# Last FFN of a cross-attention block: half of the output product ahead, scores from unscaled rows, ranks read from PSUM, the landing awaited in the second block

## The chip, the cores and the metric

The kernel runs on one core of one Trainium2 chip. The metric is the device time in microseconds, the median of three runs. All times below are of one launch on one core.

## The reference

The reference is one transformer layer on 8 batches of 512 rows of 256 numbers, float32, in two parts.

```python
x = x + xattn(layernorm(x), ctx, ctx, mask)      # 16 heads of 16, 1024 keys, softmax, then @ w_o.T
x = x + ffn(layernorm(x))

# ffn(y), for each batch:
scores = y @ w_router                 # one number per row
_, idx = top_k(scores, 128)           # the 128 best rows of the batch
x_sel = y[idx]
h = rmsnorm(x_sel, g1); qkv = h @ W_qkv.T        # 16 heads, causal attention over the 128 rows
x_attn = softmax(q k.T / 4 + causal) v @ W_out.T
h2 = rmsnorm(x_sel + x_attn, g2)
x_ff = (silu(h2 @ W1.T) * (h2 @ W2.T)) @ W3.T    # 682 wide
out = y with rows idx set to x_sel + x_attn + x_ff
```

So a batch goes through attention, an output product with w_o, a residual sum (x1), a layer norm of x1 (y), a score and a rank for each row, a gather of 128 rows, a small attention and a gated product, and an add of the 128 new rows onto their places in the output.

## The kernel before

Batches are pipelined by hand. The attention of batch b runs in 32 steps; each step has a score product on TensorE (L439), two exponentials on ScalarE (L469) and a value product (L458). Between the steps stand, by tables that name a step for each piece (`PE_SLOT`, `ACT_SLOT`, `DVE_ORDER`), the projections of batch b+1 and the pieces of the FFN of batch b-1. There the FFN has one PSUM bank for itself, bank 7, called `MISC`.

After the attention of the last batch nothing is left to hide its FFN behind. It runs as a chain of pieces, in the order of `PE_FFN`, `ACT_FFN`, `DVE_FFN` and `POOL_FFN`, with banks from `BANK_LAST`. The pieces, each named by a string, are:

- `wo0`, `wo1`: the output product. Each waits for both halves of `o_t` (the transposed attention output, two halves of 128 channels, L551), makes two of the four row tiles, and VectorE adds them to x1 (L615), takes statistics (L619) and aggregates them (L623).
- GpSimd `var`: two small instructions (L763, L765) that make the reciprocal standard deviation `rstd2`.
- `y`: VectorE subtracts the mean and multiplies by `rstd2` (L629), then multiplies by the router's weights with a running sum (L633), which gives `score`.
- `spread`: TensorE transposes the scores so that every partition holds all 512 (L247); ScalarE copies them to `all_scores` in SBUF (L496).
- `rank0` to `rank3`: VectorE counts for each row the rows ahead of it (L643, L646) and makes the selection (L605). Ahead of them stand three instructions that check denominators (L974 to L979).
- `gather`, `hidT`, `kq`, `v`, `fs`, `pv`, `wout`, `hid2T`, `u0`, `w0`, `u1`, `w1`, `down`: gather of 128 rows, keys and queries in one bank (L679, L681 read them), values, small attention, and the gated product. `u` goes through tanh on ScalarE (L522) and L716 on VectorE, `w` through L723.
- `add`: GpSimd issues an indirect DMA that adds 128 rows to the output in DRAM (L780), and waits for its landing (L782).

`product` (L256) splits a product into four column strips of 32; an fp32 product shows as two instructions for each matmul in the trace. `spare_products` (L266) are products of a constant with itself whose result nobody reads; `SPARE` says how many stand ahead of which piece on TensorE. `take_bank` (L271) waits for a bank.

The program has two blocks. The first, fast one ends with the wait of SyncE for the landing of the last indirect DMA, and all engines meet (L802). In the second each engine loads a flag; if it is set, the whole computation is done again in a general form. Here it isn't set, and the engines branch over the code to the end, where they meet again (L1061).

## Time and profile before

| | |
|---|---|
| median of 3 runs | 920.99 us (918.51, 920.99, 922.82) |
| the profiled execution | 918.08 us |
| its span, first to last instruction | 915.8 us |
| mean granted TensorE clock | 0.995 |
| TensorE busy / VectorE / ScalarE / GpSimd | 95% / 35% / 62% / 10% |
| steps of the last attention end at | 849.45 us |
| last DMA issue on GpSimd | 906.18 to 907.84 us |

About 2.3 us of the profiled execution lie around the span. The shares of busy time are of the whole span; the change touches the last 66 us of it, where TensorE is busy for a good part with spare products. In the page, the digits of TensorE's clock are 9 (0.9 or more of full speed) in all but the last of 40 slices.

### The profile page before, as it was taken

To read this page: it belongs to the slowest core of one execution; us is meant where nothing else is said; L and a number is where in the kernel's file an instruction comes from. 1 tells how busy PE (TensorE), PEld (TensorE's weight loads), DVE (VectorE), ACT (ScalarE), POOL (GpSimd) and SP (SyncE) were. 2 spreads that over 40 slices of the span, in tenths; PEclk is the share of its full clock that TensorE was granted. 3 is DMA by queue.
4 is the path that set the end of the run, shared out by engine and by line. 5 is a ranking of instruction groups with operands and counts; after the bars stand their busy time and mean duration, and the time that the engine had idled before them with its cause. 6 is when DMAs were issued, how large, how long until landed. Compare 5 with 4: busy or idle time off the path is not lost. (4 is left out here: it accounts for less than half of the span.)

```text
span 915.8 us, 28668 instructions
## 1 busy us (share of the span) xinstructions
PE 866.5 (95%) x12040; PEld 305.6 (33%) x12047; DVE 316.4 (35%) x919; ACT 570.8 (62%) x645; POOL 92.7 (10%) x147
## 2 busy tenths in 40 slices
PE   7999999999999999999999999999999999989874
PEld 2322222333333423334323433334323332324443
DVE  2222216331452216331363324532263314421631
ACT  3466777666577666766676666676676667776110
POOL 3100101110000101011101101001011100010011
PEclk9999999999999999999999999999999999999998
DMA  5060201120001200111001200202001100100000
GB/s 179 2 236 1 76 3 25 48 77 8 2 25 48 77 7 25 48 31 48 8 24 48 77 8 2 68 5 78 7 2 47 31 8 1 48 1 5 5 25 9
DMA packets 24955, 33.73 MB, mean 37 GB/s; under 512 B 1231, under 2 KB 22009, under 8 KB 24825
## 3 DMA queue, kind: packets, MB, share of 16 engines
q1 hardware_dynamic: 23672, 30.81, 10.4%
q0 software_dynamic: 1152, 1.05, 1.0%
q8 instruction: 98, 1.61, 0.7%
q14 instruction: 33, 0.26, 0.1%
HBM read 26.61 MB, written 5.24 MB: 35 GB/s over the span
## 5 line engine op out<-in xcount | busy, mean ns | idle before, releaser
L469 ACT ACTIVATE probs<-pair_bank 128x1024 f32<-128x1024 f32 x512 | 496.3, 1021 | 241.2 <-ACTq L468 241.2
L439 PE MATMUL pair_bank<-q_sb,k_sb 32*64 32x512 f32 x4096 | 286.2, 612 | 17.1 <-PEq L436 17.0
L458 PE MATMUL o_bank<-probs,va 128*32 128x512 f32 x2048 | 272.8, 604 | 3.3 <-PEq L455 2.2
L439 PEld LDWEIGHTS pair_bank<-q_sb,k_sb 32*64 32x64 f32 x4096 | 61.3, 129 | 147.2 <-issue 147.1
L458 PEld LDWEIGHTS o_bank<-probs,va 128*32 128x32 f32 x2048 | 41.3, 108 | 207.0 <-issue 122.3
L256 PE MATMUL m_bank<-wv_sb,ctx_in 128*32 128x256 f32 x1024 | 61.3, 379 | 0.4 <-PEq L271 0.4
L256 PE MATMUL m_bank<-ctx_in,wk_sb 128*32 128x512 f32 x480 | 58.1, 592 | 0.0
L542 DVE STREAM_TRANSPOSE o_blk<-o_bank 128x512 f32<-128x512 f32 x32 | 22.9, 717 | 93.8 <-DVEq L541 93.8
L595 DVE TENSOR_SCALAR q_sb<-m_bank,parity 128x512 f32<-128x512 f32 x30 | 21.1, 746 | 81.0 <-DVEq L593 81.0
L256 PEld LDWEIGHTS m_bank<-wv_sb,ctx_in 128*32 128x32 f32 x1024 | 33.9, 110 | 35.8 <-issue 20.4
L583 DVE TENSOR_SCALAR va<-m_bank,valid 128x256 f32<-128x256 f32 x64 | 28.0, 478 | 49.9 <-DVEq L577 49.9
L256 PEld LDWEIGHTS m_bank<-hid_t,w 128*32 128x32 f32 x1392 | 39.3, 110 | 17.3 <-issue 16.6
L256 PE MATMUL m_bank<-hid_t,w 128*32 128x128 f32 x1392 | 43.4, 273 | 0.5 <-PEq L271 0.5
L266 PE MATMUL o_bank<-before 128*128 128x512 bf16 x122 | 29.7, 395 | 3.3 <-POOL before L858 2.7
L615 DVE TENSOR_TENSOR x<-x,m_bank 128x512 f32<-128x512 f32 x14 | 9.6, 688 | 61.2 <-DVEq L614 61.2
L256 PE MATMUL m_bank<-xn_t,wq_sb 128*32 128x512 f32 x240 | 30.7, 592 | 0.0
L477 ACT ACTIVATE k_sb<-m_bank 128x512 f32<-128x512 f32 x30 | 17.9, 597 | 19.4 <-ACTq L476 19.4
L755 POOL TENSOR_TENSOR mask_in<-mask_in,mask_row 128x256 int32<-128x256 int32 x32 | 22.4, 730 | 69.5 <-POOLq L752 69.5
L771 POOL TENSOR_SCALAR_AFFINE_SELECT p_f<-p_f 128x1024 f32<-128x1024 f32 x16 | 17.5, 1091 | 116.4 <-POOLq L769 115.4
L780 POOL DMA_INDIRECT out_dram<-att,row_of x8 | 13.3, 1668 | 150.1 <-POOLq L779 150.1
L256 PEld LDWEIGHTS m_bank<-ctx_in,wk_sb 128*32 128x32 f32 x480 | 15.7, 110 | 35.8 <-issue 35.8
L256 PE MATMUL m_bank<-wo,o_t 128*32 128x256 f32 x448 | 26.7, 379 | 0.0
(164 smaller groups left out, 595.6 us busy)
## 6 DMA issues: line engine op xcount, KB each, us to landing
ctx_in<-in_ctxT SPq DMA_DIRECT2D x8, 1024.0 KB, 5.0
x_in<-in_x SPq DMA_DIRECT2D x8, 512.0 KB, 4.0
x<-in_x SPq DMA_DIRECT2D x8, 512.0 KB, 4.3
mask_in<-in_mask SPq DMA_DIRECT2D x8, 512.0 KB, 3.9
out_dram<-base SPq DMA_DIRECT2D x8, 512.0 KB, 5.2
mask_row<-in_mask SPq DMA_DIRECT2D x8, 128.0 KB, 3.9
wqkv<-in_wqkvT SPq DMA_DIRECT2D x1, 768.0 KB
w<-in_w1T SPq DMA_DIRECT2D x1, 682.0 KB
```

The costliest lines, as they stand in the source:

```text
L256: last = nc.tensor.matmul(dst[j], a[:, j], c, start=(begins and n == 0), stop=(ends and n == len(pairs) - 1))
L266: last = nc.tensor.matmul(dst, before[:, 0, 0:P], before[:, 1], start=True, stop=True)
L439: last = nc.tensor.matmul(pair_bank[pairs[r // 2]][j:j + 64, r % 2], key_tile(b, s, r)[:, j:j + 64], query_tile(b, s, r), start=True, stop ...
L458: last = nc.tensor.matmul(o_bank[32 * r:32 * r + 32], va[b % 2][:, t, HV * h:HV * h + 32], probs[s % 2][:, r], start=(t == 0), stop=(t == ...
L469: nc.scalar.activation(probs[s % 2][:, 2 * e:2 * e + 2, :], pair_bank[p][:], ACT.Exp, scale=HD ** -0.5).then_inc(s_free[p], 1)
L477: nc.scalar.activation(k_sb[b % 2][:, m, half * 512:(half + 1) * 512], bank[i], ACT.Copy).then_inc(bank_free[i], 1)
L542: nc.vector.transpose(o_blk[:], o_bank[:]).then_inc(o_free, 1)
L583: last = nc.vector.tensor_scalar(by_head(va[b % 2][:, t])[:, :, 0:HD], bank[i][:, e * D:(e + 1) * D].rearrange("p (h d) -> p h d", h=H), o ...
L595: last = nc.vector.tensor_scalar(q_sb[b % 2][:, m, par], bank[i], parity[:, par:par + 1], None, ALU.mult)
L755: last = nc.gpsimd.tensor_tensor(mask_words[:, t * WORDS:(t + 1) * WORDS], mask_words[:, t * WORDS:(t + 1) * WORDS], first, ALU.subtract)
L771: last = nc.gpsimd.affine_select(out=half, in_=half, compare_op=ALU.is_ge, fill=0.0, base=0, pattern=[[0, H8], [1, CAP]], channel_multipli ...
L780: nc.gpsimd.indirect_dma_start(out.rearrange("b s d -> (b s) d"), bass.IndirectOffsetOnAxis(row_of[:, 0:1], 0), att[:], None, compute_op=A ...
```

## The change

In the last FFN alone:

- `wo` takes the place of `wo0` and `wo1`. It waits for the first half of `o_t`, multiplies it with all four tiles into four banks, then waits for the second half and completes them. VectorE adds and takes statistics tile by tile.
- `score` takes the place of `y`: the mean is subtracted ahead of the wait for `rstd2`; the score product has `rstd2` as its scalar; then the rows are multiplied by `rstd2`.
- ScalarE's `spread` is gone; the ranks read the bank (bank 4).
- Keys go to one bank and queries to the next, each with a signal of its own (`k,q`); `v` moves to bank 7.
- The gated product goes `u0`, `u1`, `w0`, `w1` rather than `u0`, `w0`, `u1`, `w1`.
- Spare products: ahead of the output product 2 for 12, ahead of `spread` 17 for 24, ahead of `gather` 27 for 36.
- `add` waits for the stored rows first and for the new rows second (this holds for all batches); in the last batch GpSimd no longer waits for the landing, and SyncE waits for it in the second block, between the load of the flag and the branch.

The general form in the second block keeps the old pieces.

```diff
-PE_FFN = ["wo0", "wo1", "spread", "gather", "hidT", "kq", "v", "fs", "pv", "wout", "hid2T", "flag", "u0", "w0", "u1",
+PE_FFN = ["wo", "spread", "gather", "hidT", "k,q", "v", "fs", "pv", "wout", "hid2T", "flag", "u0", "u1", "w0",
-SPARE = {"wo0": 12, "spread": 24, "gather": 36, "hidT": 10, "pv": 14, "wout": 6, "hid2T": 10}
+SPARE = {"wo": 2, "spread": 17, "gather": 27, "hidT": 10, "pv": 14, "wout": 6, "hid2T": 10}
 def pe_ffn(pe, stage, i, part=None):
+    if stage == "wo":
+        pe.wait_ge(o_t_ready, 1)
+        tiles = [take_bank(pe, i + t)[:, 0:D] for t in range(QT)]
+        for t in range(QT):
+            product(tiles[t], [(o_t[:, 0, t * P:(t + 1) * P], wo[:, 0])], ends=False)
+        pe.wait_ge(o_t_ready, 2)
+        pe.sem_inc(o_t_ready, -2)
+        for t in range(QT):
+            product(tiles[t], [(o_t[:, 1, t * P:(t + 1) * P], wo[:, 1])], begins=False).then_inc(done["wo"], 1)
+    elif stage == "k,q":
+        ...
+        for e in range(2):
+            dst = take_bank(pe, i + e)
+            for n in range(2):
+                first = (D if e == 0 else 0) + n * P
+                last = product(dst[:, n * CAP:(n + 1) * CAP],
+                               [(wqkv[:, c, first:first + P], hid_t[:, c]) for c in range(KC)])
+            last.then_inc(done["kq"], 1)
 def dve_ffn(dve, stage, b, i):
+    if stage == "wo":
+        ...
+        for t in range(QT):
+            dve.wait_ge(done["wo"], 1)
+            dve.sem_inc(done["wo"], -1)
+            nc.vector.tensor_tensor(x1[:, t], x1[:, t], bank[i + t][:, 0:D], ALU.add).then_inc(bank_free[i + t], 1)
+            dve.drain()
+            nc.vector.bn_stats(stats2[:, t], x1[:, t])
+        dve.drain()
+        for t in range(QT):
+            nc.vector.bn_aggr(mv2[:, t], stats2[:, t])
+        dve.drain().then_inc(var2_ready, 1)
+    elif stage == "score":
+        for t in range(QT):
+            nc.vector.tensor_scalar(y[:, t], x1[:, t], mv2[:, t, 0:1], None, ALU.subtract)
+        dve.wait_ge(rstd2_ready, 1)
+        dve.sem_inc(rstd2_ready, -1)
+        dve.drain()
+        for t in range(QT):
+            unused = ties[t // 2][:, (t % 2) * D:(t % 2 + 1) * D]
+            nc.vector.scalar_tensor_tensor(out=unused, in0=y[:, t], scalar=rstd2[:, t:t + 1], in1=wr_b[:], op0=ALU.mult,
+                                           op1=ALU.mult, accum_out=score[:, t:t + 1])
+        dve.drain().then_inc(score_ready, 1)
+        for t in range(QT):
+            nc.vector.tensor_scalar(y[:, t], y[:, t], rstd2[:, t:t + 1], None, ALU.mult)
     elif stage in ("rank0", "rank1", "rank2", "rank3"):
+        others = all_scores[:] if i == MISC else bank[i]
+        elif t == 0:
+            dve.wait_ge(done["spread"], 1)
 def pool_ffn(pool, stage, n=None):
     elif stage == "add":
+        pool.wait_ge(base_stored, 16)
+        pool.sem_inc(base_stored, -16)
         pool.wait_ge(delta_ready, 1)
         pool.sem_inc(delta_ready, -1)
-        pool.wait_ge(base_stored, 16)
-        pool.sem_inc(base_stored, -16)
         nc.gpsimd.indirect_dma_start(...).then_inc(added, 16)
-        pool.wait_ge(added, 16 * (n + 1))
-        pool.sem_inc(add_done, 1)
+        if n != B - 1:
+            pool.wait_ge(added, 16 * (n + 1))
+            pool.sem_inc(add_done, 1)
 # SyncE, end of the first block
-                sp.wait_ge(added, 16 * B)
 # SyncE, second block
                 general = sp.value_load(flags_i[0:1, 0:1], min_val=0, max_val=1)
+                sp.wait_ge(added, 16 * B)
                 with sp.If(general == 1):
```

TensorE's order from the end of the last attention (`o_bank<-probs1,va1` is its last value product) to the gather, before. `before` is the constant of the spare products; the number at a row's end counts instructions of one form.

```order
L458 MATMUL o_bank<-probs1,va1 32x512 x4
L266 MATMUL pair_bank0<-before 128x512 x12
L256 MATMUL pair_bank0<-wo,o_t 32x256 x32
L266 MATMUL o_bank<-before 128x512 x24
L247 MATMUL m_bank<-ident,score 128x128 x4
L266 MATMUL o_bank<-before 128x512 x36
L256 MATMUL pair_bank0<-y_tok,sel 32x257 x16
```

And now, on the same engine at the same place:

```order
L478 MATMUL o_bank<-probs1,va1 32x512 x4
L266 MATMUL pair_bank2<-before 128x512 x2
L256 MATMUL pair_bank0<-wo,o_t 32x256 x8
L256 MATMUL pair_bank1<-wo,o_t 32x256 x8
L256 MATMUL pair_bank0<-wo,o_t 32x256 x8
L256 MATMUL pair_bank1<-wo,o_t 32x256 x8
L266 MATMUL o_bank<-before 128x512 x17
L247 MATMUL pair_bank2<-ident,score 128x128 x4
L266 MATMUL o_bank<-before 128x512 x27
L256 MATMUL pair_bank0<-y_tok,sel 32x257 x16
```

The 32 matmuls of the output product are now two passes over four tiles, with the wait for the second half of `o_t` between the passes; 26 spare products of 72 are gone.

VectorE's order from the aggregation of the statistics (L623) to the first rank (L643), before:

```order
L623 BN_AGGR mv2<-stats2 128x2 x4
L629 TENSOR_SCALAR y_tok<-x1,mv2,rstd2 128x256 x4
L633 SCALAR_TENSOR_TENSOR ties0,score<-y_tok,wr_b 128x256 x2
L633 SCALAR_TENSOR_TENSOR ties1,score<-y_tok,wr_b 128x256 x2
L974 TENSOR_SCALAR ties0<-inv_all 128x512
L976 SCALAR_TENSOR_TENSOR ties0,checks<-inv_all,ties0 128x512
L979 TENSOR_REDUCE checks<-differs 128x1
L643 SCALAR_TENSOR_TENSOR ties0,rank<-all_scores,score,before 128x128
```

And now:

```order
L639 BN_AGGR mv2<-stats2 128x2 x4
L644 TENSOR_SCALAR y_tok<-x1,mv2 128x256 x4
L650 SCALAR_TENSOR_TENSOR ties0,score<-y_tok,rstd2,wr_b 128x256 x2
L650 SCALAR_TENSOR_TENSOR ties1,score<-y_tok,rstd2,wr_b 128x256 x2
L654 TENSOR_SCALAR y_tok<-y_tok,rstd2 128x256 x4
L1039 TENSOR_SCALAR ties0<-inv_all 128x512
L1041 SCALAR_TENSOR_TENSOR ties0,checks<-inv_all,ties0 128x512
L1044 TENSOR_REDUCE checks<-differs 128x1
L695 SCALAR_TENSOR_TENSOR ties0,rank<-pair_bank2,score,before 128x128
```

Four instructions that multiply y by `rstd2` have come in between the score and the first rank (L654), and the ranks' input is a bank.

## Rows read from the trace of the kernel before

**Rows 1.** Windows by stage: length, busy time of each engine, granted clock, DMA.

```profile
845.00:916.00 71.00, 49.11 (x628) 26.46 (x634) 26.08 (x82) 8.67 (x14) 7.58 (x10) 0.94 0.06 13
```

**Rows 2.** Timeline, output product: start, length, engine, line, operation; idle time before.

```profile
851.27 0.71 DVE L551 STREAM_TRANSPOSE o_t<-o_nrm 128x512 f32<-128x512 f32 x1
852.28 3.66 PE L256 MATMUL pair_bank<-wo,o_t 128*32 128x256 f32 x64
854.39 0.69 DVE L615 TENSOR_TENSOR x<-x,pair_bank 128x512 f32<-128x512 f32 x1 [2.41 <-DVEq L614]
855.16 0.76 DVE L619 BATCH_NORM_STATS2 stats<-x 128x6 f32<-128x256 f32 x2
...
857.72 0.38 DVE L623 BATCH_NORM_AGGREGATE mv<-stats 128x2 f32<-128x6 f32 x4
```

**Rows 3.** Timeline, normalisation and scores.

```profile
858.80 1.05 POOL L765 TENSOR_TENSOR rstd<-veps,neg_half 128x4 f32<-128x4 f32 x1 [0.24 <-issue]
860.00 1.38 DVE L629 TENSOR_SCALAR y_tok<-x,mv,rstd 128x256 f32<-128x256 f32 x4 [1.90 <-DVEq L627]
861.45 0.43 DVE L633 SCALAR_TENSOR_TENSOR ties<-y_tok,wr_b 128x256 f32<-128x256 f32 x1
...
862.84 0.08 DVE L633 DVE_READ_ACCUMULATOR ties<-y_tok,wr_b 128x1 f32 x1
```

**Rows 4.** Timeline, from the spread scores to the gather.

```profile
863.25 0.62 PE L247 MATMUL m_bank<-ident,score 128*128 128x128 f32 x4 [2.02 <-PEq L271]
...
863.71 7.93 PE L266 MATMUL o_bank<-before 128*128 128x512 bf16 x35
864.00 0.60 ACT L496 ACTIVATE all_scores<-m_bank 128x512 f32<-128x512 f32 x1 [14.63 <-ACTq L495]
...
864.79 0.35 DVE L643 SCALAR_TENSOR_TENSOR ties<-all_scores,score,before 128x128 f32<-128x128 f32 x1 [0.43 <-DVEq L640]
...
869.58 0.77 DVE L605 TENSOR_SCALAR sel<-iota_r,rank 128x128 f32<-128x128 f32 x2
871.57 1.95 PE L256 MATMUL pair_bank<-y_tok,sel 128*32 128x257 f32 x32
```

**Rows 5.** One line's instructions: ns min/median/max, first and last start; forms.

```profile
L580 DVE COPY va<-valid x64: 167/174/706, 23.7 to 668.1; 128x16 f32<-128x16 f32 x64
```

**Rows 6.** Timeline, gathered rows, keys and queries.

```profile
875.88 0.48 DVE L670 SCALAR_TENSOR_TENSOR hid<-x_sel,ms,g_b 128x256 f32<-128x256 f32 x1 [0.55 <-DVEq L669]
...
877.92 1.95 PE L256 MATMUL pair_bank<-hid_t,wqkv 128*32 128x128 f32 x64 [0.84 <-PEq L271]
...
880.04 0.42 DVE L679 COPY k_f<-pair_bank 128x256 f32<-128x256 f32 x1 [2.36 <-DVEq L678]
```

**Rows 7.** Timeline, gated product.

```profile
901.41 3.23 PE L256 MATMUL pair_bank<-w,gate 128*32 128x256 f32 x48
902.03 0.56 DVE L723 SCALAR_TENSOR_TENSOR gate<-pair_bank,silu 128x384 f32<-128x384 f32 x1 [0.30 <-DVEq L722]
```

**Rows 8.** Timeline, the end.

```profile
904.81 0.42 DVE L738 TENSOR_TENSOR att<-att,pair_bank 128x256 f32<-128x256 f32 x1 [2.23 <-DVEq L737]
...
906.18 1.66 POOL L780 DMA_INDIRECT out_dram<-att,row_of  x1 [12.20 <-POOLq L779]
```

**Rows 9.** Single lines of the queues: ns min/median/max, first and last start.

```profile
L783 POOLq EVENT_SEMAPHORE  x8: 17/17/17, 227.9 to 910.1; - x8
...
L1161 POOLq TENSOR_LOAD <-flags_i x1: 504/504/504, 910.5 to 910.5; - x1
...
L1240 PEldq COMPARE_BRANCH  x1: 3927/3927/3927, 911.5 to 911.5; - x1
```

**Rows 10.** Windows of TensorE: length, busy time (instructions), granted clock, DMA.

```profile
904.00:905.00 1.00, 0.64 (x11) 1.00 0.00 0
...
907.00:908.00 1.00, 0.00 (x0) 0.50 0.00 0
```

**Rows 11.** Timeline, the first spare products of the program.

```profile
2.66 3.69 PE L266 MATMUL o_bank<-before 128*128 128x512 bf16 x9 [2.66 <-POOL before L858]
```

More of the change, by code:

```diff
@@ L45 @@
 BANK_FIRST = {"xT0": 0, "xT1": 1, "K00": 2, "Q0": 3, "K01": 4, "valid": MISC}
-BANK_LAST = {"wo0": 0, "wo1": 1, "spread": 7, "gather": 0, "hidT": 7, "kq": 0, "v": 1, "pv": 7, "wout": 0,
+BANK_LAST = {"wo": 0, "spread": 4, "rank0": 4, "rank1": 4, "rank2": 4, "rank3": 4, "gather": 0, "hidT": 7, "k,q": 0, "v": 7, "pv": 7, "wout": 0,
              "hid2T": 1, "flag": 6, "u0": 7, "w0": 0, "u1": 1, "w1": 2, "down": 3}
@@ L78 @@
 POOL_ORDER = [("F", "var"), ("P", "var"), ("F", "rms0"), ("F", "causal"), ("F", "rms1"), ("P", "differ"), ("F", "add")]
-PE_FFN = ["wo0", "wo1", "spread", "gather", "hidT", "kq", "v", "fs", "pv", "wout", "hid2T", "flag", "u0", "w0", "u1",
+PE_FFN = ["wo", "spread", "gather", "hidT", "k,q", "v", "fs", "pv", "wout", "hid2T", "flag", "u0", "u1", "w0",
           "w1", "down:0", "down:1"]
-ACT_FFN = ["spread", "hidT", "v", "fs", "hid2T", "u0", "u1"]
-DVE_FFN = ["wo0", "wo1", "y", "rank0", "rank1", "rank2", "rank3", "gather", "base", "kq", "pv", "wout", "check", "u0", "w0", "u1", "w1",
+ACT_FFN = ["hidT", "v", "fs", "hid2T", "u0", "u1"]
+DVE_FFN = ["wo", "score", "rank0", "rank1", "rank2", "rank3", "gather", "base", "k,q", "pv", "wout", "check", "u0", "u1", "w0", "w1",
            "down"]
 POOL_FFN = ["var", "rms0", "causal", "rms1", "add"]
-SPARE = {"wo0": 12, "spread": 24, "gather": 36, "hidT": 10, "pv": 14, "wout": 6, "hid2T": 10}
+SPARE = {"wo": 2, "spread": 17, "gather": 27, "hidT": 10, "pv": 14, "wout": 6, "hid2T": 10}
 SPARE_FIRST = 18
@@ L637, in dve_ffn @@
                 t = int(stage[4])
-                if t == 0:
+                others = all_scores[:] if i == MISC else bank[i]
+                if t == 0 and i == MISC:
                     dve.wait_ge(all_ready, 1)
                     dve.sem_inc(all_ready, -1)
+                elif t == 0:
+                    dve.wait_ge(done["spread"], 1)
+                    dve.sem_inc(done["spread"], -1)
                 ahead, behind = slice(0, (t + 1) * P), slice(t * P, S)
-                nc.vector.scalar_tensor_tensor(out=ties[0][:, ahead], in0=all_scores[:, ahead], scalar=score[:, t:t + 1],
+                nc.vector.scalar_tensor_tensor(out=ties[0][:, ahead], in0=others[:, ahead], scalar=score[:, t:t + 1],
                                                in1=before[:, t, ahead], op0=ALU.is_ge, op1=ALU.mult,
                                                accum_out=rank[:, t, 0:1])
-                nc.vector.scalar_tensor_tensor(out=ties[1][:, behind], in0=all_scores[:, behind], scalar=score[:, t:t + 1],
+                nc.vector.scalar_tensor_tensor(out=ties[1][:, behind], in0=others[:, behind], scalar=score[:, t:t + 1],
                                                in1=before[:, t, behind], op0=ALU.is_gt, op1=ALU.is_gt,
@@ L675, in dve_ffn @@
                 dve.drain().then_inc(base_ready, 1)
+            elif stage == "k,q":
+                dve.wait_ge(done["kq"], 1)
+                dve.sem_inc(done["kq"], -1)
+                nc.vector.tensor_copy(k_f[:], bank[i][:, 0:D].rearrange("p (m k) -> p m k", m=M2)).then_inc(bank_free[i], 1)
+                dve.wait_ge(done["kq"], 1)
+                dve.sem_inc(done["kq"], -1)
+                for par in range(2):
+                    last = nc.vector.tensor_scalar(q_f[:, :, par], bank[i + 1][:, 0:D].rearrange("p (m k) -> p m k", m=M2),
+                                                   parity[:, par:par + 1], None, ALU.mult)
+                last.then_inc(bank_free[i + 1], 1)
+                dve.drain().then_inc(kq_sb, 1)
             elif stage == "kq":
@@ L970, in _ @@
                 dve.drain()
-                for stage in ("wo0", "wo1", "y"):
+                for stage in DVE_FFN[:2]:
                     dve_ffn(dve, stage, B - 1, BANK_LAST.get(stage, MISC))
@@ L980, in _ @@
                 dve.drain()
-                for stage in DVE_FFN[3:]:
+                for stage in DVE_FFN[2:]:
                     dve_ffn(dve, stage, B - 1, BANK_LAST.get(stage, MISC))
```

14 lines of the change are left out of this document (11 added, 3 removed).

## The prediction

> **What bounds the kernel now.** I looked at the stages first. In the last 71 us TensorE is busy for 49 us, ScalarE for 9, VectorE for 26 [rows 1]; no engine is full, and a good part of TensorE's 49 is spare products. This stretch is a chain of single pieces, so only what stands on the chain counts, each piece by its duration and the hand-over behind it. Then I read the timeline of the stretch piece by piece, and last the queues' own lines after the last DMA. The other 845 us are not touched: the tables of steps stay, and in the loop only the order of two waits of `add` changes, the first of which has long been satisfied. The reader should see three things. The output product's 3.66 us run behind the second half of `o_t`, and VectorE stands 2.41 us before its first sum [rows 2]. VectorE stands 1.90 us for `rstd2`, and only then makes y [rows 3]. And between the end of GpSimd's DMA instruction at 907.84 and the load of the flag at 910.5 nothing works; everybody waits for the landing, seen at 910.1 [rows 8, 9]. The branch of TensorE's queue, 3.93 us, comes behind that [rows 9].
>
> All sums are against the profiled execution: 918.08 us, of which 915.8 are its span. The median is 2.91 above it (920.99); I put the same saving on both.
>
> **Output product.** Before, all 64 instructions stand behind `o_t`'s second half: 3.66 us, less the last one's 0.38, is 0.051 each [rows 2]. Now 32 are done ahead. Two spare products and these take some 2.1 us from 849.6, so they end by 851.8, before `o_t` at 851.98: hidden. The second pass starts about as before, perhaps 0.1 earlier since the banks are already taken: 852.18. Tile 0 is complete 7 x 0.051 + 0.38 later, and VectorE follows in 0.12: 853.05, for 854.39 before. From there VectorE is the bound. A sum of 128x256 costs 0.42 [rows 8], the drain 0.08, one piece of statistics 0.38 (half of 0.76 [rows 2]), the next wait some 0.07: 0.95 a tile, four tiles 3.8, where before two sums of 0.69 and their statistics stood. The aggregation starts at 856.9 for 857.72: **0.85 gained**, between 0.5 and 1.2 by the unseen pitch of the tiles (0.87 to 1.05).
>
> **Scores.** Before, from the end of the wait: 1.38 for y, 0.07, then four score products [rows 3]. The four subtractions now run in the 1.90 us of the wait for GpSimd, and one more drain of 0.05 comes in: 1.40 gained. The score product gets a scalar read from SBUF; L670, of that form, takes 0.48 [rows 6] where L633 takes 0.43 [rows 3]: four times 0.055 lost. Net 1.18 if GpSimd is left alone. It may not be. In the batches' loop L580, a VectorE copy from SBUF to SBUF, takes 174 ns as a rule and up to 706 [rows 5], the long ones while GpSimd's L755 runs (23.4 to 25.5 us): each holds up the other. The trace has no case in which VectorE begins first and goes on. Bounds: 0, and the whole of four subtractions, 1.1. I take 0.3, about one subtraction, since the two GpSimd instructions are short. **0.88 gained** (0.1 to 1.3).
>
> The Trainium skill's page "SBUF — State Buffer" (SBUF: two separate sides) says that VectorE in a two-port mode and GpSimd share a port pair by an exclusive lock, held for a whole instruction by whoever starts first. The slow copies agree with it. Taken at its word, a row of four subtractions without a gap keeps GpSimd out till the last, which is the first rival below; if it lets go between them, 0.3 is about right.
>
> **Ranks and gather.** The copy on ScalarE goes, but VectorE now has four multiplications by `rstd2` between the score and the checks. They cost 1.38 at y's price (two scalars), 1.1 if one scalar makes them as much cheaper as the score product got dearer; I take 1.2. Before, the first rank came 1.87 after the last score (862.92 to 864.79), with 0.43 idle [rows 3, 4], 0.22 of it only the wait for the copy. Now: 1.87 - 0.22 + 1.2 = 2.85. The ranks take 5.56 (864.79 to 870.35), which I leave: silu and gate read PSUM at 0.55 for 384 numbers [rows 7], no dearer than SBUF; the bound above is 0.05 each, 0.4. So the selection ends 8.41 after the score, and TensorE can begin 0.3 later, at 8.71. Before it began 8.65 after the score [rows 4]: the selection was there at 7.43, but 36 spare products ran to 871.6. With 27 they end at 0.33 + 0.62 + 27 x 0.22 = 6.9. The stall by spare products goes, and VectorE is late in its place: **0.05 lost** (0.5 lost to 0.2 gained).
>
> **Keys and queries.** The keys are complete after half of 1.95 us plus a tail, at 879.0 rather than 879.9, so their copy (0.42, of which 0.34 stood ahead of the queries) lies beside the second half [rows 6]: **0.34 gained**.
>
> **Gated product.** With u1 ahead of w0, silu 1 is done by 900.4 and the last gate can start when w1 is complete, at 901.8 for 902.03 [rows 7]. But gate 0 comes at 900.7 to 901.3, not 899.4 to 900.0, and `down:0` waits for it: 901.63 for 901.41. Its and the second half's 48 instructions need 2.97 without a gap (0.054 each and 0.38), and end at 904.60, for 904.64 [rows 7]. **0.04 gained**: the stall moves from the second half to the first.
>
> **End.** One semaphore fewer between the new rows and the DMA: **0.10**. Then GpSimd goes on at 907.84 instead of 910.1 and all engines meet some 0.4 later, so the flag is loaded at 908.25 for 910.5: **2.25 gained**. The landing, at 910.1 less the other gains, is then hidden by the branch of 3.93 us [rows 9]; SyncE needs under 0.5 after it. Bounds: 0 if GpSimd's drain waits for the landing, 2.4.
>
> **Sum.** 0.85 + 0.88 - 0.05 + 0.34 + 0.04 + 0.10 + 2.25 = 4.41 us. The profiled execution would come to 913.7, the median to 920.99 - 4.41 = **916.6 us**, 0.48% less. About 0.5%, 4.6 us, is what a measurement of this kernel can tell from no change; I stand nearly on that line.
>
> **Rivals.**
> 1. *VectorE keeps GpSimd out* until all four subtractions are over: 1.1 lost instead of 0.3, 917.4. For it: the slow copies [rows 5]. Against: they got in between GpSimd's instructions each time.
> 2. *The landing isn't hidden*: GpSimd's drain, or the code that the branch needs, waits for the DMA. The 2.25 are gone: 918.8. Nothing shows a drain right behind the DMA; for the change speaks that the DMA instruction is over 2.2 us before the landing.
> 3. *All gaps close well*: no conflict (0.3), tiles at 0.87 (0.35), ranks 0.15: 915.8.
> 4. *TensorE's clock falls; slower.* TensorE ends the output product near 854.2 and 17 spares by 858.0; the scores come at about 861.5. That is 3.5 us idle, where before 2.0 left the clock at full [rows 4]. At the end it was still 1.00 with the last work in 904 to 905, and 0.50 from 907 [rows 10]: 2.4 of 2.4 GHz, then 1.2. So the fall is rather likely here. What does it cost? At the start of the program the spare products come at the low clock, about 0.43 us apart, and after some 3.2 us at 0.22 [rows 11]. Three us of it cost 1.5 of spare products, and TensorE has 1.8 to spare before the gather: nothing. It decides from about 3.6 us of low clock on. If the clock stays down from the scores to the gather's end, 27 x 0.21 + 1.95 + 0.5 - 1.8 = 6.3 us are lost: 922.9, slower than before; through the keys, values and the gated product some 14 us more. For it: the fewer spares; against: they are dense behind the scores.
>
> The Trainium skill's page "TensorE: Matmul & The Clock Gate" (What's actually happening) says the throttled clock is the default and activity lifts it, so that any long pause is followed by a slow start. The end of the trace agrees. By it the fall comes, and so does the recovery under the 27 spare products.
>
> **How the numbers follow.** Forecast 0.50 (own range 915.6 to 917.6, two in five of it under 916.4), rival 1 0.10, rival 2 0.11, rival 3 0.17, rival 4 with a cost 0.12, half of which is over 0.5% slower. Faster by over 0.5%: 0.20 + 0.17 and a little of the scatter of three runs, 0.40. Slower by over 0.5%: 0.06. Within: 0.54. Range: from rival 3 with favourable runs, 913.0, up past rival 2 to part of rival 4, 921.0.
>
> **What would show it.** The first residual sum starts near 853.05 and there are four; GpSimd's first small instruction begins within 0.2 us of the aggregation's end, or 1.1 later (rival 1); the first rank comes about 2.85 after the last score; the gather starts 0.3 behind the selection, not behind spare products; keys are copied beside the queries' product; `down` runs without a gap; the flag's load comes about 0.4 behind the DMA instruction's end. I am wrong if the 2.25 at the end isn't there, or if the granted clock is 0.5 at the gather.

## The result, and the profile after

| | before | after |
|---|---|---|
| median of 22 runs each, same chip | 919.76 us (916.96 to 924.28) | 916.68 us (914.26 to 921.06) |
| ratio, 95% interval | | 0.9962 [0.9949, 0.9976] |
| span of the profiled execution | 915.8 us | 914.6 us |
| last attention product ends at | 849.45 | 851.06 |
| from there to the end | 66.31 us | 63.55 us |

The kernel became 0.38% faster (0.24 to 0.51%), under the 0.5% that the prediction took as what can be told from no change. The forecast of 916.6 us is met to 0.1 us, but not by its own sum. That subtracted 4.41 us from a median of three runs, 920.99; over 22 runs before has 919.76, and the gain is 3.08 by the medians and 2.76 by the last stretch of the two profiles. The prediction's largest term, the 2.25 us of the landing, is missing.

The spans differ by only 1.2 us since the untouched attention came out 1.6 us longer in this execution (the last section has the reason), so everything below is counted from the end of the last attention product. Stages of that last stretch, in us from there (e1, e3, e6, e7 and e11 are experiments, told below):

| | before | after | gained in the step | predicted | e1 | e3 | e6 | e7 | e11 |
|---|---|---|---|---|---|---|---|---|---|
| aggregation starts | 8.27 | 7.02 | 1.25 | 0.85 | 7.01 | 8.27 | 7.01 | 7.02 | 7.01 |
| last score ends | 13.47 | 11.26 | 0.96 | 0.88 | 11.26 | 13.48 | 11.26 | 11.27 | 11.26 |
| first rank starts | 15.34 | 14.07 | | | 14.06 | 15.34 | 12.71 | 14.07 | 12.71 |
| selection ends | 20.89 | 19.62 | | | 19.61 | 20.90 | 18.26 | 19.62 | 18.26 |
| gather starts on TensorE | 22.12 | 19.96 | -0.05 | -0.05 | 19.94 | 21.23 | 18.59 | 19.95 | 18.59 |
| score products of the FFN | 32.30 | 29.80 | 0.34 | 0.34 | 29.79 | 31.41 | 28.45 | 29.80 | 28.44 |
| new rows complete | 55.78 | 53.22 | 0.06 | 0.04 | 53.22 | 54.53 | 51.90 | 53.50 | 52.11 |
| last DMA instruction starts | 56.73 | 54.07 | 0.10 | 0.10 | 54.07 | 55.48 | 52.75 | 54.35 | 52.96 |
| GpSimd loads the flag | 61.03 | 58.19 | 0.18 | 2.25 | 58.40 | 59.76 | 56.87 | 54.36 | 52.97 |
| end | 66.31 | 63.55 | -0.08 | 0 | 63.87 | 65.12 | 62.26 | 59.93 | 58.32 |

Where two kernels have the same code up to a mark, their marks agree to 0.02 us as far as the score products (after, e1 and e7) or the selection (before and e3), so terms of a tenth can be read there from one execution each. Behind the score products they can't: from there to the new rows after and e1 take 23.42 us and e7 takes 23.70, and before takes 23.48 where e3, with the same code in that stretch, takes 23.12. The sum is 1.25 + 0.96 - 0.05 + 0.34 + 0.06 + 0.10 + 0.10 = 2.76.

The output product and the statistics of after, from its timeline (start, length, engine, line, operation; idle time before), against [rows 2]:

```profile
852.88 0.71 DVE L571 STREAM_TRANSPOSE o_t<-o_nrm 128x512 f32<-128x512 f32 x1
...
853.74 1.93 PE L256 MATMUL pair_bank<-wo,o_t 128*32 128x256 f32 x32 [0.28 <-PEq L320]
854.55 0.42 DVE L634 TENSOR_TENSOR x<-x,pair_bank 128x256 f32<-128x256 f32 x1 [0.96 <-DVEq L633]
855.06 0.43 DVE L636 BATCH_NORM_STATS2 stats<-x 128x6 f32<-128x256 f32 x1
855.41 0.40 DVE L634 TENSOR_TENSOR x<-x,pair_bank 128x256 f32<-128x256 f32 x1
...
858.08 0.38 DVE L639 BATCH_NORM_AGGREGATE mv<-stats 128x2 f32<-128x6 f32 x4
858.63 1.14 DVE L644 TENSOR_SCALAR y_tok<-x,mv 128x256 f32<-128x256 f32 x4 [0.17 <-issue]
858.70 0.38 POOL L828 TENSOR_SCALAR veps<-mv 128x4 f32<-128x4 f32 x1 [11.18 <-POOLq L827]
859.31 1.11 POOL L830 TENSOR_TENSOR rstd<-veps,neg_half 128x4 f32<-128x4 f32 x1 [0.24 <-issue]
860.62 0.48 DVE L650 SCALAR_TENSOR_TENSOR ties<-y_tok,rstd,wr_b 128x256 f32<-128x256 f32 x1 [0.84 <-DVEq L646]
...
862.45 1.14 DVE L654 TENSOR_SCALAR y_tok<-y_tok,rstd 128x256 f32<-128x256 f32 x4
862.66 0.62 PE L247 MATMUL pair_bank<-ident,score 128*128 128x128 f32 x4 [3.21 <-PEq L271]
863.12 5.99 PE L266 MATMUL o_bank<-before 128*128 128x512 bf16 x27
```

VectorE's wait for the first sum fell from 2.41 to 0.96 us, and only half of the product (1.93 us for 3.66) stands behind `o_t`. The four subtractions now run beside GpSimd's two instructions, in the time that stood idle. GpSimd was not kept out: it begins 0.07 behind the first subtraction. L830 takes 1.11 where it took 1.05 [rows 3].

The way to the gather, from the same timeline, against [rows 4]:

```profile
865.13 0.35 DVE L695 SCALAR_TENSOR_TENSOR ties<-pair_bank,score,before 128x128 f32<-128x128 f32 x1 [0.18 <-DVEq L692]
...
869.92 0.77 DVE L625 TENSOR_SCALAR sel<-iota_r,rank 128x128 f32<-128x128 f32 x2
871.02 1.95 PE L256 MATMUL pair_bank<-y_tok,sel 128*32 128x257 f32 x32 [1.91 <-PEq L271]
```

TensorE now waits 1.91 us for the selection. Before, the gather followed the spare products with no wait.

The end, as single lines of the queues (ns min/median/max, first and last start), against [rows 9]:

```profile
L868 POOLq DRAIN  x1: 4144/4144/4144, 904.9 to 904.9; - x1
...
L1227 POOLq TENSOR_LOAD <-flags_i x1: 508/508/508, 909.2 to 909.2; - x1
...
L1308 PEldq COMPARE_BRANCH  x1: 3837/3837/3837, 910.4 to 910.4; - x1
```

GpSimd has no wait for the landing in its code any more, and stands as long as before all the same. A drain is the instruction by which the program lets an engine wait for its own earlier work, and every engine ends a block with one. On GpSimd this one takes 4.14 us and ends at 909.05; the last DMA has landed at 908.97. In before the same drain came behind the explicit wait and took 0.13 us.

### The profile page after: what moved, and what is told of

It reads as the page before. It is cut to its first block and busy times, and to the rows that moved or that the text cites. A ratio compares the mean times of both kernels' runs of the same rounds, so it can differ in the third digit from the quotient of the medians.

```text
span 914.6 us, 28632 instructions
## 1 busy us (share of the span) xinstructions
PE 864.2 (94%) x12021; PEld 304.3 (33%) x12021; DVE 317.7 (35%) x925; ACT 570.2 (62%) x644; POOL 92.9 (10%) x147
## 3 DMA queue, kind: packets, MB, share of 16 engines
q0 software_dynamic: 1152, 1.05, 1.0%
q8 instruction: 98, 1.61, 0.7%
```

## The experiments

Each kernel was run beside the kernel before on the same chip; a ratio is to that. The kernel before had medians of 919.93 (beside e1 to e4), 920.74 (e5, e6, e7, e9) and 920.78 (the others), so kernels are to be compared by their ratios. Edits of the second block that follow from a move are left out of the cuts of code. The marks in us are from the end of the last attention product, as in the table.

**e1, the landing awaited where it was.**

```diff
 # SyncE, end of the first block
+                sp.wait_ge(added, 16 * B)
 # GpSimd, add: for all batches
-                if n != B - 1:
-                    pool.wait_ge(added, 16 * (n + 1))
-                    pool.sem_inc(add_done, 1)
+                pool.wait_ge(added, 16 * (n + 1))
+                pool.sem_inc(add_done, 1)
```

> The changed kernel with the landing awaited where it was: GpSimd waits for its last DMA and SyncE waits in the first block. Theory (GpSimd's drain at the end of the block waits for the landing by itself): 0.1 to 0.3 us slower than the changed kernel, the flag loaded 4.3 us behind the start of the last DMA instruction (4.1 in the changed kernel). Rival (the move of the wait did bring its 2.25 us, and the profiled execution is an odd one): 2.0 to 2.4 us slower.

916.75 us, ratio 0.9960 [0.9949, 0.9972], the same as after. GpSimd loads the flag at 58.40 for 58.19, and the end is 0.32 later. Moving the wait was worth 0.2 to 0.3 us here, not 2.25.

**e2, a drain behind each indirect DMA.**

```diff
         nc.gpsimd.indirect_dma_start(...).then_inc(added, 16)
+        pool.drain()
```

> The changed kernel with a drain of GpSimd right behind each of the eight indirect DMAs, ahead of the wait for the landing. Theory (a drain behind such a DMA ends with its landing): the seven new drains in the loop last 3.6 us or more, and each ends within 0.2 us of the last landing of its DMA, also where a landing is late. Rival (the drain of 4.1 us belongs to the end of the block, or is a fixed cost of making descriptors): drains of under 0.6 us, or of one length whatever the landing.

```profile
L847 POOLq DRAIN  x8: 4116/4209/4372, 226.4 to 908.3; - x8
```

All eight drains take over 4.1 us, and each ends 0.08 us behind the landing of its DMA (of the first: landed 230.69, drain over at 230.77). So a drain of GpSimd behind an indirect DMA is a wait for its landing, at any place of the program. The one execution took 920.03 us.

**e3, the kernel before with 27 spare products ahead of the gather.**

```diff
-SPARE = {"wo0": 12, "spread": 24, "gather": 36, ...}
+SPARE = {"wo0": 12, "spread": 24, "gather": 27, ...}
```

> The kernel before with 27 spare products ahead of the gather instead of 36, nothing else. Theory (before, TensorE came to the gather late for its spare products): gather 0.3 us behind the selection instead of 1.2, so 0.9 us faster than before (0.7 to 1.1). Rival (the gather waited for something else): no change, under 0.2.

Timeline of TensorE in e3, against [rows 4]:

```profile
865.13 0.62 PE L247 MATMUL m_bank<-ident,score 128*128 128x128 f32 x4 [2.03 <-PEq L271]
865.58 5.99 PE L266 MATMUL o_bank<-before 128*128 128x512 bf16 x27
872.55 1.95 PE L256 MATMUL pair_bank<-y_tok,sel 128*32 128x257 f32 x32 [0.98 <-PEq L271]
```

918.95 us, ratio 0.9983 [0.9967, 0.9998]. The gather starts at 21.23 for 22.12, 0.33 behind the selection: nine spare products were holding back the kernel before by 0.89 us, a third of what the last stretch gained by the whole change. The end came 1.19 earlier, over the 0.7 to 1.1 expected; 0.36 of that lies between the score products and the new rows, where the code is the same, and is scatter.

**e4, the changed kernel with 24 and 36 spare products.**

```diff
-SPARE = {"wo": 2, "spread": 17, "gather": 27, ...}
+SPARE = {"wo": 2, "spread": 24, "gather": 36, ...}
```

> The changed kernel with the old numbers of spare products, 24 ahead of the spread and 36 ahead of the gather. Theory (in the changed kernel VectorE is late for the gather, so the spare products have room): 36 of them end at about 871.1 where the gather began at 871.0, so 0.1 to 0.4 us slower than the changed kernel; the 24 end before the scores come. Rival (the fewer spare products are themselves worth what they were worth before): 0.9 us slower or more. If a clock that falls in the 3.2 us pause cost anything, this kernel would be faster.

916.09 us, ratio 0.9969 [0.9955, 0.9983]. The gather starts at 19.95 for 19.96. In the changed kernel the nine more spare products cost the gather nothing, not even the 0.1 to 0.4 expected, since the scores, and so the spare products behind them, come 2.2 us earlier while VectorE does not keep up with that. The profile's end, at 64.09, is 0.54 later than in after; all of it lies behind the score products (24.01 us from them to the new rows), where the code is the same.

**e5, the old order of scaled rows and scores.**

```diff
-DVE_FFN = ["wo", "score", "rank0", ...]
+DVE_FFN = ["wo", "y", "rank0", ...]
```

> The changed kernel with one part undone: y is made after the wait for rstd2 with both scalars, as before, and then the scores; the ranks still read the bank. Theory (the rearranged score moves 4 instructions from ahead of the score to behind it, and both places are on VectorE's chain): score 0.96 later, but first rank 1.5 to 1.65 behind it instead of 2.81, so selection and gather 0.1 to 0.3 us earlier than in the changed kernel, and the time 0 to 0.3 us less. Rival (the time saved in the wait for rstd2 reaches the end): 0.9 us slower than the changed kernel.

917.75 us, ratio 0.9965 [0.9948, 0.9982]. Scores end at 12.22 for 11.26, but the first rank starts at 13.86 and the selection ends at 19.41, 0.21 *earlier* than in after. So the new order of VectorE gains 0.96 us at the scores, loses more than that through the four multiplications, and gives nothing to the selection. What it gives shows up elsewhere: in e5 the gather started at 21.27, 1.86 behind the selection, with TensorE like this (timeline, and windows with the granted clock as second column after the busy time):

```profile
863.53 1.09 PE L247 MATMUL pair_bank<-ident,score 128*128 128x128 f32 x4 [4.16 <-PEq L271]
864.41 7.91 PE L266 MATMUL o_bank<-before 128*128 128x512 bf16 x27
872.25 1.51 PE L256 MATMUL pair_bank<-y_tok,sel 128*32 128x257 f32 x24
```

```profile
860.00:861.00 1.00, 0.00 (x0) 1.00 0.00 0
862.00:863.00 1.00, 0.00 (x0) 0.50 0.00 0
868.00:869.00 1.00, 1.00 (x6) 0.86 0.00 0
870.00:871.00 1.00, 1.00 (x6) 1.00 0.00 0
```

The clock fell to 1.2 GHz inside the pause of 4.16 us, the spread scores took 1.09 for 0.62, and the 27 spare products 7.91 for 5.99; they, not VectorE, were last. I had not expected that. (A gather of fewer than 32 instructions is cut off by the end of the view, here and below; where one spare product is missing from a count, so is its record.) The profile ends at 65.34, 1.79 later than after's, but the ratio is within 0.0003 of after's 0.9962: this cost is seen in the one profile and not in the runs.

**e6, the checks behind the last rank.**

```diff
-                # tensor_scalar, scalar_tensor_tensor, tensor_reduce on inv_all and differs, here ahead of rank0
                 for stage in DVE_FFN[2:]:
                     dve_ffn(dve, stage, B - 1, BANK_LAST.get(stage, MISC))
                     dve.drain()
+                    if stage == "rank3":
+                        # the same three instructions
```

> The changed kernel with the three checks of denominators moved from ahead of the first rank to behind the last, into VectorE's wait for the gather. Theory (VectorE bounds the stretch from score to gather): selection 1.3 to 1.45 us earlier, and the time 1.2 to 1.45 us less than the changed kernel. Rival (the 27 spare products or the spread of the scores become the bound at once): 0 to 0.4 us less.

916.90 us, ratio 0.9952 [0.9934, 0.9970]. The first rank starts at 12.71 for 14.07, selection and gather come 1.36 earlier (18.26, 18.59), and the end 1.29. The profile confirms the theory; a comparison of medians alone could not have told 0.0010 of ratio apart.

**e7, one block.** The work of the first block stands at the head of each engine's part of the second; VectorE signals the flag, and each engine waits for that alone.

```diff
-            block = ctx.enter_context(nc.Block())
-            @block.sync
-            def _(sp):
+            def first_sync(sp):
 # and so for the other four engines; VectorE's last drain:
+                dve.drain().then_inc(flag_set, 1)
 # second block, each engine ahead of the load of the flag
+                first_sync(sp)
+                sp.wait_ge(flag_set, 1)
```

> The changed kernel as one block: each engine goes on from its first part to the load of the flag when VectorE has set it, without the meeting of all engines between; only the meeting at the very end waits for GpSimd's drain. Theory (the drain waits for the landing, so the flag's load and the branch of 3.9 us must stand ahead of the meeting with GpSimd): the flag is loaded at about the start of the last DMA instead of 4.1 us behind it, the branch ends some 5.1 us behind the DMA's start, and the kernel is 3.7 to 4.1 us faster than the changed one. Rival (the branch's code comes late whatever stands ahead, or loads behind the DMA): under 1 us.

910.91 us, ratio 0.9898 [0.9867, 0.9930]. In the profiled execution the end is at 59.93 for 63.55: 3.62 us, a little under the expected 3.7. By the ratios e7 is 0.64% below after, some 5.9 us; with five runs its interval reaches up to 0.9930, which would be 2.9, so the 3.62 of the profile stands within it. The queues' lines of e7:

```profile
L1313 PEldq COMPARE_BRANCH  x1: 4158/4158/4158, 910.4 to 910.4; - x1
```

```profile
L1121 POOLq DRAIN  x1: 3650/3650/3650, 910.7 to 910.7; - x1
L1121 DVEq DRAIN  x1: 65/65/65, 913.3 to 913.3; - x1
L1121 SPq DRAIN  x1: 7/7/7, 914.4 to 914.4; - x1
L1121 PEldq DRAIN  x1: 68/68/68, 914.6 to 914.6; - x1
```

TensorE's branch of 4.16 us and the landing now lie beside each other and end together, at 914.6 and 914.3. GpSimd's drain ends at 914.3 too, so it followed the landing although that came later than in after. This is what the change meant to do. It does not quite hide the landing, for that became longer. The DMA view of the last stretch, after first, then e7:

```profile
DMA packets 144, 0.13 MB, mean 25 GB/s; under 512 B 16, under 2 KB 144, under 8 KB 144
...
out_dram<-att,row_of POOLq DMA_INDIRECT x1, 3.8
```

```profile
DMA packets 149, 0.18 MB, mean 30 GB/s; under 512 B 16, under 2 KB 144, under 8 KB 144
## 3 DMA queue, kind: packets, MB, share of 16 engines
q0 software_dynamic: 144, 0.13, 19.9%
q14 instruction: 4, 0.03, 1.9%
q8 instruction: 1, 0.02, 1.7%
issues: line engine op xcount, KB each, median us to landing
out_dram<-att,row_of POOLq DMA_INDIRECT x1, 4.9
```

Five instruction packets, the code behind the branches, run in among the 144 packets of the DMA. One of them, of 16 KB, takes 1.66 us from 2.03 behind the DMA's start. The bulk of the DMA's packets is over at 3.5 behind its start in both kernels; the last ones come at 4.45 rather than 3.49. That they stand behind that packet on one DMA engine is argued from those times, not shown.

**e8, one block and an early flag.** As e7, with VectorE's flag ahead of `u0`.

```diff
                 for stage in DVE_FFN[2:]:
+                    if stage == "u0":
+                        # wait for done["flag"], three comparisons, tensor_reduce, then flag_set
```

> The changed kernel in one block, as in the earlier run of one block (end 59.93 us behind the last attention product), with VectorE's flag computed before the gated product instead of at the end, so TensorE branches 2.7 us earlier, before the last indirect DMA starts. Theory: in the run of one block the last DMA landed 4.9 us after its start instead of 3.8, since the queues' code loads (16 KB packets) run among its 144 packets; the landing ends the program with TensorE's branch just beside it. Moving the flag takes 0.6 us of VectorE's flag work away from before its branch; the load of VectorE's code starts 0.6 earlier but still falls into the DMA: landing 4.9 to 5.3 behind its start, end 59.8 to 60.3, no gain over one block alone. Rival: TensorE's branch, not the landing, was the end there: then the end is 0.3 to 1 us earlier (59.0 to 59.6) and the landing 3.8 behind the DMA's start.

912.26 us, ratio 0.9901 [0.9875, 0.9927]. TensorE branches at 52.51 and is through at 55.9, before the landing, which stays 4.83 behind the DMA's start. The end is at 59.68, between the two ranges but with the landing where the theory had it: 0.25 gained, and the landing with its meeting is what is left.

**e9, everything at once.** One block, early flag, late checks, the multiplications of y on ScalarE, 22 spare products ahead of the gather.

```diff
-                for t in range(QT):
-                    nc.vector.tensor_scalar(y[:, t], y[:, t], rstd2[:, t:t + 1], None, ALU.mult)
+                dve.drain().then_inc(y_read, 1)
+            if stage == "scale":      # ScalarE
+                act.wait_ge(y_read, 1)
+                for t in range(QT):
+                    nc.scalar.activation(y[:, t], y[:, t], ACT.Copy, scale=rstd2[:, t:t + 1])
+                act.drain().then_inc(y_scaled, 1)
+                    if stage == "gather":   # TensorE, ahead of the spare products
+                        pe.wait_ge(y_scaled, 1)
```

> A version with all of it: one block, the flag made ahead of u0 where VectorE waits, the checks behind the last rank, y scaled by ScalarE (idle there) rather than by VectorE, 22 spare products ahead of the gather. Theory: selection 2.4 us earlier than in the changed kernel; end bounded by the landing of the last DMA, 3.9 us behind its start, and 0.4; 7.2 to 7.8 us faster than the changed kernel. Rival (the earlier flag brings nothing, the branch of TensorE still bounds): 6.2 to 6.6 us faster.

912.21 us, ratio 0.9905 [0.9878, 0.9931]: far from the 7.2 us or more expected against after, and no better than e7. The profile ends at 60.38, 3.17 before that of after. The timeline of e9 shows a part of what is missing:

```profile
866.04 1.71 ACT L517 ACTIVATE y_tok<-y_tok,rstd 128x256 f32<-128x256 f32 x4 [11.50 <-DVEq L659]
866.22 0.62 PE L248 MATMUL pair_bank<-ident,score 128*128 128x128 f32 x4 [3.21 <-PEq L272]
866.99 0.35 DVE L700 SCALAR_TENSOR_TENSOR ties<-pair_bank,score,before 128x128 f32<-128x128 f32 x1 [1.10 <-DVEq L697]
...
867.82 6.61 PE L267 MATMUL o_bank<-before 128*128 128x512 bf16 x22 [0.98 <-ACTq L518]
...
871.77 0.77 DVE L631 TENSOR_SCALAR sel<-iota_r,rank 128x128 f32<-128x128 f32 x2
...
874.36 0.86 PE L257 MATMUL pair_bank<-y_tok,sel 128*32 128x257 f32 x12
```

With the multiplications gone VectorE waits 1.10 us for the spread scores, so the first rank comes only 0.34 earlier than in e6, not 1.1. The spare products had to wait for ScalarE and then met the low clock; the gather started 1.82 behind the selection. So the selection gained 0.7 us less than expected and the gather lost 1.5 more. The rest lies behind them: 24.20 us from the score products to the new rows for 23.42, and the landing 5.29 behind the DMA's start for the 3.9 expected.

**e10, one block and late checks, 24 spare products.** The edits of e6 and e7, and:

```diff
-SPARE = {"wo": 2, "spread": 17, "gather": 27, ...}
+SPARE = {"wo": 2, "spread": 17, "gather": 24, ...}
```

> The changed kernel with two edits: the two checks of the ranks behind the last rank (as in the run of the late checks, selection 1.36 us earlier there) and all work in one block, so that each engine goes from its last instruction to the flag and its branch without the meeting of all engines (end 3.62 us earlier there). 24 spare products before the gather instead of 27. If both gains add, the end of the profile stands 4.9 to 5.1 us closer to the last attention product than in the changed kernel (58.5 instead of 63.55) and the median is 4.5 to 5.5 below its level, about 912 here. Rival: the checks now stand before the gather with no cover, or TensorE's clock falls in the pause before the spread scores as it did in two of nine profiles that had this pause or a longer one; then the 24 spares come at half pace, end after the selection, and the gather starts 1 to 1.8 behind the selection instead of 0.33: 1 to 1.5 of the 5 are lost in that execution.

911.78 us, ratio 0.9895 [0.9869, 0.9921]. The end is at 58.44, 5.11 before that of after. The selection ends at 18.27, but the gather starts at 19.01: the clock had fallen at 863.40, behind the pause, and the 24 spare products took 7.03 us. (The expectation's "two of nine" was short: e1, e5 and e9 had a fall there, three of the seven earlier profiles with this pause or a longer one.) Both theory and rival hold, and the rival's price is 0.42 us.

**e11, the same with the pause filled.**

```diff
-SPARE = {"wo": 2, "spread": 17, "gather": 24, ...}
+SPARE = {"wo": 2, "spread": 28, "gather": 24, ...}
```

> The run before with one number changed: 28 spare products instead of 17 while the scores are awaited (11 more at 0.22 us fill 2.4 of TensorE's 3.2 us pause). Theory: the fall of the granted clock comes from that pause; no fall is seen between the attention and the end of down, the gather starts 0.3 behind the selection, and the median is the same as in the run before or up to 1 us lower (by the share of executions in which it fell there). Rival: the fall has nothing to do with the pause (there are stretches at half clock inside the dense attention work too): a fall can be seen here as well, and the median is the same. Second rival: the spares end after the scores and push the spread scores back: first rank later by 0.1 to 0.6.

```profile
863.19 0.62 PE L247 MATMUL pair_bank<-ident,score 128*128 128x128 f32 x4 [0.83 <-PEq L271]
863.65 5.34 PE L266 MATMUL o_bank<-before 128*128 128x512 bf16 x23
870.19 1.08 PE L256 MATMUL pair_bank<-y_tok,sel 128*32 128x257 f32 x16 [1.20 <-PEq L271]
```

911.29 us, ratio 0.9888 [0.9863, 0.9913], the lowest ratio of all kernels here, though those of e7 to e10 lie within its interval (and e7 has the lower median, 910.91). No fall behind the pause, the gather at 18.59, the first rank not pushed back.

**e12, the old scores with the pause filled.**

```diff
-SPARE = {"wo": 2, "spread": 17, "gather": 27, ...}
+SPARE = {"wo": 2, "spread": 31, "gather": 27, ...}
-DVE_FFN = ["wo", "score", "rank0", ...]
+DVE_FFN = ["wo", "y", "rank0", ...]
```

> The changed kernel with the old scores of scaled rows (TensorE's pause is 4.2 us, the clock fell in it at 861.46 and the gather started 1.86 behind the selection instead of 0.33), with 31 spare products instead of 17 while the scores are awaited (14 more at 0.22 us fill 3.1 of the pause). Theory: the clock stays at 1.00 and the gather starts 19.7 us behind the last attention product instead of 21.27; median 1.0 to 1.6 lower than the one with the empty pause. Rival (clock not tied to the pause): the same fall, the same 21.3, the same median.

```profile
865.50 0.62 PE L247 MATMUL pair_bank<-ident,score 128*128 128x128 f32 x4 [1.14 <-PEq L271]
865.96 5.99 PE L266 MATMUL o_bank<-before 128*128 128x512 bf16 x26
872.69 1.68 PE L256 MATMUL pair_bank<-y_tok,sel 128*32 128x257 f32 x25 [0.74 <-PEq L271]
```

917.25 us, ratio 0.9957 [0.9941, 0.9974]. The profile is as the theory had it: clock at 1.00, gather at 19.74, 1.53 earlier than in e5. The medians differ by 0.50, and the intervals of the two ratios overlap almost wholly; the expected 1.0 to 1.6 is not shown, though intervals of this width do not rule it out. Either the clock does not fall in every execution of e5, or single profiles differ; that stays open.

## Why the prediction was right, and where not

**Output product (0.85; 1.25).** The mechanism held, VectorE is the bound from the first sum on. The size was off by the pitch of the tiles and the start. The first sum came 3.49 us behind the last attention product, 0.11 before the 3.60 of the sum, and the tiles come every 0.84 us, just under the lower bound of 0.87, since a sum behind the drain overlaps the end of the statistics (0.43 long, the next sum 0.35 behind its start). The first sum starts 1.67 behind the start of `o_t`'s transposition, where the whole product made it 3.12 [rows 2].

**Scores (0.88; 0.96).** Here the sum has the mechanism and nearly the size. The clash with GpSimd is in it: 0.38 and 1.11 us for its two instructions, 0.15 and 0.06 more than in before. Rival 1, VectorE keeping GpSimd out for 1.1, is refuted. Its ground was weak already in [rows 5]: the prediction says of VectorE's slow copies and GpSimd's L755 that "each holds up the other", but all 32 instructions of L755 take 0.72 to 0.74 us, so only VectorE was held. Rival 3 came in part, in the pitch of the tiles (0.84 where it had 0.87).

The rule of the Trainium skill's page "SBUF — State Buffer" (SBUF: two separate sides) is an exclusive lock on the port pair, held for one instruction. The prediction stretched this to a whole row of instructions when it said "taken at its word". The trace agrees with the rule as the page states it, with the lock let go between instructions: four subtractions without a gap held up GpSimd by 0.21 in all.

**Ranks and gather (-0.05; -0.05).** First rank 2.81 behind the last score for the 2.85 of the sum, gather 8.70 for 8.71. e3 shows the other half of the argument: in before the gather stood behind spare products by 0.89. e5 adds what the sum did not say: of the score's gain nothing reaches the selection. The four multiplications took 1.14 and the wait that they replaced was short. If the two VectorE edits are looked at alone they gain nothing up to the selection (-0.21); of the 2.16 up to the gather 1.27 are already there at the selection, as much as at the aggregation (1.25), and 0.89 are spare products that had stood too long.

**Keys and queries (0.34; 0.34 with the gather's own rest), semaphore (0.10; 0.10).** As predicted.

**Gated product (0.04; 0.06).** The number was met, but it is less than the same code scatters by, so no gain is shown. The second half (`down`) gained 0.41 and the first lost 0.35, as if the stall had moved. But a part of before's 3.23 us for `down` is a gap of 0.29 that e3, with the same code, does not have; and all twelve profiles with the new order have a gap of 0.24 to 0.79 us in TensorE's weight loads within u and w. First before, then after:

```profile
903.14 1.02 PEld L256 LDWEIGHTS pair_bank<-w,gate 128*32 128x32 f32 x23 [0.29 <-issue]
```

```profile
898.73 2.11 PEld L256 LDWEIGHTS pair_bank<-hid_t,w 128*32 128x32 f32 x76 [0.25 <-issue]
```

From the score products to the new rows the new order takes 23.4 to 24.2 us, the old one 23.48 (before) and 23.12 (e3): by these the new order is not faster. What makes the gaps stays open.

**Landing (2.25; 0.10 to 0.18). This is the step that failed.** The sum let GpSimd go on when its DMA instruction ends, and let all engines meet 0.4 later. In fact GpSimd's drain at the end of the block holds it until the data have landed, at any place (e2). It was named as rival 2, with a chance of 0.11, and by the prediction's own sign ("I am wrong if the 2.25 at the end isn't there") this part is wrong; "nothing shows a drain right behind the DMA" was true of the trace, where an explicit wait stood ahead of the drain, and should have made it an open bound, not a small chance. e1 puts the move at 0.2 to 0.3 us. In e7, with the meeting itself gone, the end is 3.62 earlier and the landing does lie beside the branch. It was the block's end, not the wait in it, that had to go.

**Clock (rival 4).** In the profile of after it stayed at 1.00 through a pause of 3.21 us. In e1 and e8, with the same pause and the same 27 spare products, it fell behind it and the gather still started at 19.94 and 19.95. So the prediction's answer, that three us at the low clock are covered, holds; the price of 6.3 us never came. In e1 it holds narrowly: the spare products ended at 19.72. The fall has a price once VectorE is faster (e10, 0.42) or the pause longer (e5, about 1.5), each seen in one profile. Over the profiles: pauses of 3.2 us ahead of the spread scores, 4 falls in 8 (e1, e8, e9, e10; not in after, e2, e6, e7); 4.2 us, 1 in 1; up to 2.1 us, none in 5 (before, e3, e4, e11, e12). That speaks for the pause as the cause but doesn't show it: a profile like e11's, without a fall, would come about half of the time with the pause of 3.2 us too.

The Trainium skill's page "TensorE: Matmul & The Clock Gate" (What's actually happening) has the throttled clock as the default, which activity releases; the prediction took from it that any long pause is followed by a slow start. For 3.2 us a fall came in half of the profiles, and the clock fell 0.5 to 1.9 us behind the pause, under the spare products, not in it. The recovery came under them as well in all of them, as the page says.

So the total was right by luck. The gain was 1.33 us short (4.41 forecast, 3.08 by the medians): of the landing 2.15 did not come, the other terms brought 0.50 more, and the medians have 0.32 more than the profiles. The median of three runs before, from which it was subtracted, was 1.23 above that of 22, and that made up for it. Rival 2, put at 918.8, is what happened in the kernel.

## What to carry to other kernels

Taking an explicit wait away helps only if nothing behind it waits for the same event: on the engine that issues an indirect DMA, the drain at the end of a block is such a wait, so look for one with a single extra drain before you count the gain. When a chain is shortened on one engine, ask which engine was last at the next meeting: here all of the 0.96 us at the scores was paid back by work moved behind them, and a third of the gain was nine filler products too many in the kernel before. And filler has two sides, a price when it runs past the wait and a price when it leaves the engine idle so long that the rest may run at the low clock. Filling the pause and keeping the part behind it short cost nothing in e11; that it gains time is seen in single profiles, not in the medians. Last, let the same code run in two kernels before you trust a small term: the 0.06 us of the gated product looked like a forecast met.

## What the runs showed of the hardware

- A drain of GpSimd behind an indirect DMA of 128 rows took 4.12 to 4.37 us and ended 0.08 us behind the landing, 8 times of 8.
- The same DMA lands 3.8 us behind its start when nothing else runs, and 4.7 to 5.3 (e7 to e11) when the code behind the branches is loaded meanwhile. Such packets don't delay it each time: the sixth DMA of the loop has an instruction packet of 8 KB and one of 16 KB beside it and landed after 5.51 us in before, 4.17 in after and 3.94 in e2.
- TensorE's granted clock drops to half for 3.4 us also inside the dense attention work. Windows of after show one:

```profile
603.00:604.00 1.00, 1.00 (x15) 0.50 0.00 0
606.00:607.00 1.00, 1.00 (x24) 1.00 0.00 0
```

  In the kernel before the window at 603 had 1.00. From one value product near 598.3 to the one 128 on it took 54.20 us in after and 52.56 in before: these 1.64 us are about what the attention of after came out longer by (1.61). Such stretches come at few places: one begins between 601.8 and 606.0 us in eight of the fourteen profiles, one between 26.8 and 29.1 in six, and three lie elsewhere. The attention ends at 848.9 to 850.6 us in profiles with none, 851.0 to 852.0 with one, 853.0 and 854.2 with two, 854.6 and 855.0 with three (e9 and e7). The runs that were not profiled fit, by the mean granted clock that is on record for each: of the 22 runs of after the three lowest (0.987 to 0.989) have spans of 916.4 to 919.1 us, the four highest (0.994 to 0.997) 912.3 to 913.3. So most of the scatter of 3 to 8 us between runs of one kernel, which is as large as the whole change, goes with the clock. Why it falls there stays open.
